# The first experts' tile table computed earlier and partly on GpSimd, its second running sum as one scan, one routing step moved by four slots and one load cut in three

## The chip, the cores and the metric

The kernel runs on one core of one Trainium2 chip. Its engines are TensorE (PE in the rows, its weight loads PEld), VectorE (DVE), ScalarE (ACT), GpSimd (POOL) and SyncE (SP, which issues most of the DMAs). The metric is the time of one execution in device microseconds, as the median of several runs: 1346.81 us for the kernel before (3 runs, 1345.29 to 1347.44).

## The reference

One decoder layer in fp32 on x of 4 x 512 x 256, with a context of 4 x 1601 x 256. Cut to what matters:

```python
x = x + self_attention(layernorm(x))            # 16 heads of 64, causal, with a relative bias
x = x + cross_attention(layernorm(x), context)  # 16 heads of 16, 1601 keys, RMS-normed q and k
# mixture of experts on h = layernorm(x), 2048 tokens
scores = softmax(h @ classifier.T)              # 40 classes: 32 experts and 8 of which each passes h on
top6 = top_k(scores + correction_bias, 6)       # six classes a token
for e in range(32):
    y[e] = (silu(h @ Wg[e].T) * (h @ Wu[e].T)) @ Wd[e].T
x = x + 2.5 * (sum over a token's experts of scores * y, and h * sum of its passing classes' scores)
```

## The kernel before

The three stages run one after the other, and each engine has its own program, written out in order; semaphores tie them. Nothing is scheduled by a planner at run time: what stands earlier on an engine is done earlier, and a wait holds all that stands behind it.

**Cross attention.** Each batch of 512 tokens takes 52 slots: 4 groups of 4 heads by 13 blocks of 128 keys. In slot s PE multiplies scores for slot s (L1226), then probabilities by values for slot s - 2 (L1241), then does one side job that a list gives the slot (PLAN, or ROUTE in the last two batches); ACT takes the exponential of the slot's scores in two pieces (L1387). At the end of a group DVE copies the sums out of PSUM (L1660), PE transposes them (L1153, side job "o"), DVE divides (L1586, L1590), and POOL adds them to x (L1063). PE's side job waits for the copy of the group before.

**Routing beside it.** While the last batch is in cross attention, the tokens of batches 0 to 2 are routed in side jobs (ROUTE): "rx" transposes the normalised tokens (L1160), "rl" multiplies them by the classifier (L1169), "rk" ranks each token within its expert (L1177, L1179). DVE normalises (L91 to L99), picks six classes (L1480 to L1507), and packs the rows with places and weights (L1513 to L1530, the function pack). POOL then sends the packed rows to HBM, sorted by expert, in 24 indirect DMAs a batch (L1033), in the order of the slots.

**The experts.** Batch 3 can be routed only when its cross attention has ended. That is the stretch on which most of the change bears: layer norm on DVE, transposes (L1964) and classifier (L1970) on PE, softmax and top six on DVE and ACT, the mask of picked classes (L2111), running counts over the four blocks of 128 tokens (L2120), two sums over the partitions on PE (L1975 for batches 0 to 2, L1976 for all), and from these the tile table. The expert stage works on 128 tiles of 128 rows; the first 40 (EARLY) hold rows of batches 0 to 2 alone, so they can start while batch 3's rows are still being sent. DVE works out for each tile its expert and its first row: tiles per expert, running sums over the 32 experts by five shifted additions (L2138), and then, one tile to a partition, the entry of the table (L2143 to L2166). PE spreads it (L1984), and DVE writes it as integers, "steer" (L2169). Only then does SP load rows (L1886 reads the table, L1887 loads). DVE packs batch 3's rows after that (L2176 to L2189), and POOL sends them (L1946).

keep_busy is a number of matmuls (L1957) whose result nobody reads. SP loads the last expert weights when x is complete (L1856, L1873). In the tile loop PE turns a tile (L1995), multiplies (L2007, L2016), with copies and silu on ACT (L2054, L2061, L2076), products on DVE (L2209, L2216), and an indirect DMA of the result by POOL (L1938). Six row tiles may be under way (X_RING). At tile 40 SP waits until batch 3's rows are sent and loads the tokens of batches 0 to 2 (acc, L1881), which are needed only at the end, when the six parts of each token are summed.

## Time and profile before

| | |
|---|---|
| median of 3 runs | 1346.81 us |
| the profiled execution | 1349.23 us |
| its span, first to last instruction | 1347.5 us |
| mean granted clock of TensorE in it | 0.972 of full speed |
| self attention, then cross attention, until | 1061.8 us |
| routing of batch 3, until the table is there | 1086.4 us |
| tile loop, until | about 1300 us |
| sums and output, until | 1347.5 us |
| busy share of PE, DVE, ACT, POOL | 91%, 53%, 64%, 52% |

The limits of the stages were read from the timeline. The clock columns are the share of full speed that was granted to TensorE: 1.00 is 2.4 GHz and 0.50 is 1.2 GHz. A row of a timeline gives start, duration, engine, line and operation, and in brackets how long the engine had been idle and for whom it waited. The whole profile's busy shares say little here: the routing of batch 3 is a chain of short instructions on one engine after the other, in which no engine but PE, with its keep_busy, looks busy.

### The profile page before, as it was taken

To read this page: it belongs to the slowest core of one execution; us is meant where nothing else is said; L and a number is where in the kernel's file an instruction comes from. 1 tells how busy PE (TensorE), PEld (TensorE's weight loads), DVE (VectorE), ACT (ScalarE), POOL (GpSimd) and SP (SyncE) were. 2 spreads that over 40 slices of the span, in tenths; PEclk is the share of its full clock that TensorE was granted. 3 is DMA by queue.
4 is the path that set the end of the run, shared out by engine and by line. 5 is a ranking of instruction groups with operands and counts; after the bars stand their busy time and mean duration, and the time that the engine had idled before them with its cause. 6 is when DMAs were issued, how large, how long until landed. Compare 5 with 4: busy or idle time off the path is not lost.

```text
span 1347.5 us, 27953 instructions
## 1 busy us (share of the span) xinstructions
PE 1232.5 (91%) x8788; PEld 761.1 (56%) x8788; DVE 716.3 (53%) x2370; ACT 865.8 (64%) x1691; POOL 695.8 (52%) x775
## 2 busy tenths in 40 slices
PE   5999999999999885899999999999989899899955
PEld 4666776776676474433333333333322589799954
DVE  6666466557555557563136313632553366566647
ACT  4666456546645425668977897789989447577730
POOL 1776557557656602355217611762377447766640
PEclk9999999999999897999999999999999889899988
DMA  7976466556535621100011001010283646665649
GB/s 238 351 253 223 166 231 229 204 175 232 184 140 193 201 63 34 33 23 12 18 40 35 9 17 40 11 35 1 94 294 123 245 141 201 223 185 177 179 152 385
DMA packets 146277, 195.08 MB, mean 145 GB/s; under 512 B 12592, under 2 KB 133056, under 8 KB 145488
## 3 DMA queue, kind: packets, MB, share of 16 engines
q1 hardware_dynamic: 135376, 162.97, 36.5%
q0 software_dynamic: 10752, 30.26, 6.3%
q8 instruction: 77, 1.26, 0.4%
q14 instruction: 72, 0.59, 0.2%
HBM read 71.01 MB, written 122.18 MB: 143 GB/s over the span
## 4 chain that ended last, share of the span: by engine, by line
PE 55%; ACT 16%; issue 12%; DVE 8%; DMA 3%; POOL 3%; ACTq 2%; SPq 0%; POOLq 0%; DVEq 0%
PE sa_pf L347 11%; ACT xa_probs L1387 8%; PE xa_banks L1226 7%; PE xa_banks L1241 6%; PE sa_po L422 5%; PE sa_ps L396 5%; PE xa_banks L1109 5%; PE sa_ptr L407 5%; PE sa_pf L380 4%; ACT mo_xs_t L2054 3%; DMA mo_w_all<-parts 2%; ACTq L2058 2%; PE mo_banks L2007 2%; ACT mo_silu L2076 1%; PE mo_banks L1957 1%
## 5 line engine op out<-in xcount | busy, mean ns | idle before, releaser
L1387 ACT ACTIVATE xa_probs<-xa_banks 128x1024 f32<-128x1024 f32 (+1 forms) x416 | 401.9, 1045 | 85.8 <-PE xa_banks L1226 84.9
L334 POOL TENSOR_SCALAR sa_probs<-sa_probs,sa_recip 128x128 f32<-128x128 f32 (+3 forms) x256 | 274.8, 1087 | 176.4 <-DVE sa_recip L585 176.2
L465 ACT ACTIVATE sa_probs<-sa_probs,sa_neg_max 128x128 f32<-128x128 f32 (+3 forms) x256 | 141.9, 555 | 148.0 <-DVE sa_neg_max L522 148.0
L1241 PE MATMUL xa_banks<-xa_probs,xa_v_one 128*17 128x512 f32 (+1 forms) x1664 | 219.6, 600 | 6.8 <-ACT xa_q_aug L1333 4.5
L1226 PE MATMUL xa_banks<-xa_q_aug,xa_k_aug 32*128 32x512 f32 (+1 forms) x1664 | 153.8, 443 | 13.6 <-issue 3.7
L1938 POOL DMA_INDIRECT parts<-mo_y,mo_dest x128 | 122.9, 960 | 61.8 <-issue 33.1
L2007 PE MATMUL mo_banks<-mo_xs_t,mo_gu 128*128 128x128 f32 x1024 | 138.5, 279 | 0.0
L522 DVE CUSTOM_DVE_ANT_0 sa_probs<-sa_ps,sa_toeplitz 128x128 f32<-128x128 f32 (+3 forms) x256 | 115.5, 488 | 38.7 <-PE sa_ps L396 35.9
L2007 PEld LDWEIGHTS mo_banks<-mo_xs_t,mo_gu 128*128 128x128 f32 x1024 | 128.0, 196 | 0.1
L2061 ACT ACTIVATE mo_gu<-mo_w_all 128x512 f32 x128 | 80.7, 630 | 67.6 <-issue 53.4
L1226 PEld LDWEIGHTS xa_banks<-xa_q_aug,xa_k_aug 32*128 32x128 f32 (+1 forms) x1664 | 62.0, 180 | 107.3 <-ACT xa_probs L1387 74.6
L582 DVE COPY sa_pt<-sa_ptr 128x128 f32<-128x128 f32 (+3 forms) x128 | 62.8, 490 | 103.8 <-PE sa_ptr L407 103.7
L407 PE MATMUL sa_ptr<-sa_ident,sa_probs 128*128 128x128 f32 x640 | 94.8, 276 | 6.7 <-ACT sa_pt L488 3.5
L407 PEld LDWEIGHTS sa_ptr<-sa_ident,sa_probs 128*128 128x128 f32 x640 | 75.7, 141 | 30.1 <-issue 11.5
L1033 POOL DMA_INDIRECT rows<-xa_k_area,xa_place_i x72 | 70.9, 985 | 38.4 <-issue 20.7
L969 POOL TENSOR_TENSOR xa_k_area<-xa_k_area 128x256 f32<-128x256 f32 (+1 forms) x39 | 23.9, 612 | 123.3 <-DVE xa_k_area L1558 115.8
L422 PE MATMUL sa_po<-sa_pt,sa_v 128*64 128x256 f32 (+3 forms) x512 | 85.2, 455 | 1.0 <-issue 1.0
L2016 PE MATMUL mo_banks<-mo_w_all,mo_hidden_t 128*128 x256 | 76.9, 383 | 0.4 <-DVE mo_y L2216 0.4
L1241 PEld LDWEIGHTS xa_banks<-xa_probs,xa_v_one 128*17 128x17 f32 (+1 forms) x1664 | 28.0, 95 | 85.3 <-issue 53.5
L1558 DVE TENSOR_TENSOR xa_k_area<-xa_banks,xa_bkv 128x256 f32<-128x256 f32 (+1 forms) x52 | 21.9, 424 | 101.0 <-PE xa_banks L1109 100.7
L488 ACT ACTIVATE sa_pt<-sa_ptr 128x128 f32<-128x128 f32 (+3 forms) x128 | 54.9, 429 | 32.1 <-PE sa_ptr L407 30.4
L2209 DVE TENSOR_TENSOR mo_hidden_t<-mo_banks,mo_silu 128x128 f32<-128x128 f32 x128 | 37.3, 291 | 71.5 <-ACT mo_silu L2076 66.7
(309 smaller groups left out, 2310.9 us busy)
## 6 DMA issues: line engine op xcount, KB each, us to landing
rows<-sa_blank SPq DMA_DIRECT2D x128, 548.0 KB, 3.5
mo_xs<-rows SPq DMA_DIRECT2D x128, 137.0 KB
parts<-sa_blank SPq DMA_DIRECT2D x96, 128.0 KB, 3.6
mo_w_all<-parts SPq DMA_DIRECT2D x16, 768.0 KB, 14.5
xa_raw<-in_ctx_t SPq DMA_DIRECT2D x24, 256.0 KB, 2.8
mo_w_all<-in_gate_up_p SPq DMA_DIRECT2D x2, 2816.0 KB, 17.2
sa_toeplitz<-extended_bias SPq DMA_DIRECT2D x8, 512.0 KB, 7.4
mo_w_all<-in_down_p SPq DMA_DIRECT2D x2, 2048.0 KB, 15.5
```

Of the source, the lines that this page charges most:

```text
L334: pool.tensor_scalar(probs[:, t % SLOTS, 0:w], probs[:, t % SLOTS, 0:w], recip[:, col:col + 1], None, ALU.mult).then_inc(probs_ready, 1)
L347: last = pe.matmul(out, u, v, start=(n == 0), stop=(n == 3 * chunks - 1))
L407: last = pe.transpose(ptr[t % 2][:, k * P:(k + 1) * P], probs[:, t % SLOTS, k * P:(k + 1) * P], ident[:])
L422: last = pe.matmul(po[a * DH:(a + 1) * DH, k * P:T], v_sb[:, k, h * DH:(h + 1) * DH], pt[:, pt_at(h, k, k):pt_at(h, k, TT)], start=(k == 0 ...
L465: act.activation(probs[:, t % SLOTS, 0:w], probs[:, t % SLOTS, 0:w], ACT.Exp, bias=neg_max[:, i:i + 1], scale=-1.0, accum_out=sums[:, i:i ...
L522: dve.tensor_tensor_reduce(out=probs[:, t % SLOTS, 0:w], in0=ps[t % SCORES][:, 0:w], in1=toeplitz[:, h, w - 1::-1], scale=-1.0 / DH, scala ...
L1226: last = pe.matmul(banks[0:m, 2 * ((n + i // 2) % 3) + i % 2, :], keys, q[rows, :], start=(k == 0), stop=(k == len(parts) - 1))
L1241: last = pe.matmul(banks[32 * i:32 * i + XD + 1, 6 + group % 2, :], v_one[b % 2][0:m, c, 4 * g + i, :], probs[0:m, (2 * j + i // 2) % RING ...
L1387: act.activation(probs[0:m, n % RING, :, :], banks[0:m, 2 * (n % 3):2 * (n % 3) + 2, :], ACT.Exp).then_inc(probs_ready, 1)
L1938: pool.indirect_dma_start(out=parts, out_offset=bass.IndirectOffsetOnAxis(ap=dest[:, t:t + 1], axis=0), in_=y[t % Y_RING][:], in_offset=No ...
L2007: last = pe.matmul(banks[:, 2 + t % 2, half * P:(half + 1) * P], gu[t % W_RING][:, at:at + INTER], xs_t[t % T_RING][:, c, :], start=(c == ...
L2061: act.activation(gu[t % W_RING][:], w_all[:, bass.ds(e * (KD * 2 * INTER), KD * 2 * INTER)], ACT.Copy).then_inc(gu_ready, 1)
```

## The change

- The side job "rk" of batch 1 moves from slot 15 to slot 19 of the last batch.
- The very last addition of the cross attention to x moves from POOL to DVE.
- PE transposes batch 3's raw tokens as soon as x is complete, and no longer the normalised ones. The mean is taken out afterwards, as mean times the column sum of the classifier (class_mean), and the factor rstd is applied after the largest logit is subtracted. The normalised rows are made by normalise(t), in four pieces put at other places.
- Everything in the tile table that depends on batches 0 to 2 alone moves from DVE to a new function on POOL, early_tiles, of 24 chained steps, whose input is summed by PE and copied by ACT beforehand.
- The total counts are summed by PE from the mask and the earlier counts in five accumulating matmuls, so that they don't wait for the running counts. The running sum of all tiles is one tensor_tensor_scan. What is left on DVE of the tile table is a short chain that joins both halves.
- The steering table is released before row_no is made. ACT runs one silu on a single column beforehand.
- acc is loaded in three parts, at tiles 56, 72 and 88, in place of one at tile 40.
- The numbers of keep_busy matmuls change: 24, 20, 26 and 12 before; 3, 2, 20, 8 and 16 now.

Cut to its core:

```diff
-             (B - 1, 10): ("rl", 1, 0), (B - 1, 15): ("rk", 1, 0), (B - 1, 22): ("rx", 2, 0),
+             (B - 1, 10): ("rl", 1, 0), (B - 1, 19): ("rk", 1, 0), (B - 1, 22): ("rx", 2, 0),
...
+                        if g == QUADS * B - 1:
+                            continue
...
+                    if group == QUADS * B - 1:
+                        wait_out(dve, f)
+                        cols = x_sb[:, :, (QUADS - 1) * 4 * XD:]
+                        dve.tensor_tensor(cols, cols, o_norm[:].rearrange("p t j d -> p t (j d)"), ALU.add
+                                          ).then_inc(x2_part, 1)
...
+    TOKENS_AT = {56: 0, 72: 1, 88: 2}
...
                 if t == EARLY:
                     sp.wait_ge(sent[1], 16 * TT * TOP_K)
-                    sp.dma_start(acc[:], x2.rearrange("b (t p) d -> p (b t) d", p=P)[:, 0:TT * LAST, :]
+                if t in TOKENS_AT:
+                    b = TOKENS_AT[t]
+                    sp.dma_start(acc[:, TT * b:TT * (b + 1), :], x2[b].rearrange("(t p) d -> p t d", p=P)
                                  ).then_inc(acc_in, 16)
...
+        def early_tiles(pool):
+            chain = Chain(pool, early_ready)
+            late = is_late[:].to_broadcast([P, E_ROUTED])
+            pool.memset(choice[:, :, E_ALL:], HUGE)
+            for i in range(3):
+                pool.memset(early_n[i][:, 0:ZEROS], 0.0)
+                last = pool.memset(all_n[i][:, 0:ZEROS], 0.0)
+            chain.then_wait(last)
+            pool.tensor_copy(counted[:, 0, :], picked[:].bitcast(F32))
+            chain.then_wait(pool.tensor_copy(meta[:, :, 2, :], spare_no[:]))
+            filled_n = early_n[2][:, ZEROS:]
+            pool.wait_ge(early_out, 1)
+            chain.then_wait(pool.tensor_scalar(counts[:], counts[:], 0.5 - 0.5 * P, TO_TILES, ALU.add, ALU.add))
+            chain.then_wait(pool.tensor_scalar(filled_n, counts[:], TO_TILES, 1.0 / P, ALU.subtract, ALU.mult))
+            held = early_n[2]
+            for i in range(5):
+                at = ZEROS - 2 ** i
+                chain.then_wait(pool.tensor_tensor(early_n[i % 2][:, ZEROS:], held[:, ZEROS:],
+                                                   held[:, at:at + E_ROUTED], ALU.add))
+                held = early_n[i % 2]
+            filled = held[:, ZEROS:]
+            chain.then_wait(pool.tensor_scalar(taken[:], filled, float(EARLY), None, ALU.min))
...
+            chain.then_wait(pool.tensor_scalar(early_steps[:], swap[:], float(P), float(REGION), ALU.mult, ALU.add))
...
+            return chain.n
...
         def run_gpsimd(pool):
+            kept.through(pool)
+            kept.stored(pool)
+            assert early_tiles(pool) == EARLY_STEPS
             pool.wait_ge(row_ready, 1)
...
             pe.wait_ge(const_ready, 2)
-            keep_busy(24)
-            pe.wait_ge(xn_ready, 1)
+            kept.sent_ready(pe)
+            pe.matmul(banks[:, 2, 0:E_ROUTED], ones_r[:], picked[:, 0:E_ROUTED], start=True, stop=True
+                      ).then_inc(early_psum, 1)
+            pe.wait_ge(kept.router_in, 32)
+            for c in range(KD):
+                last = pe.matmul(banks[:, 5, 0:E_ALL], ones[:], kept.cls[:, c, :], start=(c == 0), stop=(c == KD - 1))
+            last.then_inc(early_psum, 1)
+            keep_busy(3)
+            kept.through(pe)
...
+            act.wait_ge(const_ready, 2)
+            act.activation(silu[0][:, 0:1], ident[:, 0:1], ACT.Silu)
...
+            for t in range(TT):
+                last = dve.bn_stats(stats[:, t, :], own_x[:, t, :])
+            chain.then_wait(last)
+            for t in range(TT):
+                last = dve.bn_aggr(mean_var[:, t, :], stats[:, t, :])
+            chain.then_wait(last)
+            dve.wait_ge(early_psum, 2)
+            dve.tensor_tensor(class_mean[:], banks[:, 5, 0:E_ALL].unsqueeze(1).to_broadcast([P, TT, E_ALL]),
+                              mean_var[:, :, 0:1].to_broadcast([P, TT, E_ALL]), ALU.mult)
+            chain.then_wait(dve.tensor_scalar(var[:], mean_var[:, 0:TT, 1], LN_EPS, None, ALU.add))
+            rsqrt(dve, chain, rstd[:], var[:], tmp[:])
+
             dve.wait_ge(lg_psum, 1)
             logits = banks[:, 4, 0:TT * E_ALL].rearrange("p (t e) -> p t e", e=E_ALL)
-            chain.then_wait(dve.tensor_reduce(tmp[:], logits, AX.X, ALU.max))
-            dve.tensor_tensor(scores[:], logits, tmp[:].unsqueeze(2).to_broadcast([P, TT, E_ALL]), ALU.subtract
+            chain.then_wait(dve.tensor_tensor(scores[:], logits, class_mean[:], ALU.subtract))
+            chain.then_wait(dve.tensor_reduce(row_max[:], scores[:], AX.X, ALU.max))
+            chain.then_wait(dve.tensor_tensor(scores[:], scores[:], row_max[:].unsqueeze(2)
+                                              .to_broadcast([P, TT, E_ALL]), ALU.subtract))
+            dve.tensor_tensor(scores[:], scores[:], rstd[:].unsqueeze(2).to_broadcast([P, TT, E_ALL]), ALU.mult
                               ).then_inc(shifted, 1)
+            normalise(0)
...
+            dve.wait_ge(early_ready, 2)
...
+            dve.tensor_tensor(mask[:], left[:, :, 0:E_ALL], choice[:, :, 0:E_ALL], ALU.not_equal
+                              ).then_inc(mask_ready, 1)
+            dve.wait_ge(mask_ready, 1)
+            for t in range(TT - 1):
                 last = dve.tensor_tensor(counted[:, t + 1, :], counted[:, t, :].bitcast(F32),
                                          mask[:, t, :].bitcast(F32), ALU.add)
-                if t == TT - 1:
-                    last.then_inc(mask_ready, 1)
-                else:
+                if t < TT - 2:
                     chain.then_wait(last)
+            last.then_inc(counted_ready, 1)
+
+            n_tiles = all_n[2][:, ZEROS:]
+            dve.wait_ge(count_psum, 1)
+            chain.then_wait(dve.tensor_scalar(ends[:], banks[:, 7, 0:E_ROUTED], 0.5 * P - 0.5, TO_TILES,
+                                              ALU.add, ALU.add))
+            chain.then_wait(dve.tensor_scalar(n_tiles, ends[:], TO_TILES, 1.0 / P, ALU.subtract, ALU.mult))
+            all_tiles = all_n[0][:, ZEROS:]
+            chain.then_wait(dve.tensor_tensor_scan(all_tiles, ones[:, 0:E_ROUTED], n_tiles, 0.0, ALU.mult, ALU.add))
+            dve.wait_ge(early_ready, EARLY_STEPS)
+            dve.scalar_tensor_tensor(out=steps[:], in0=n_tiles, scalar=late_rows[:], in1=early_steps[:],
+                                     op0=ALU.mult, op1=ALU.add)
+            chain.then_wait(dve.scalar_tensor_tensor(out=ends[:], in0=all_tiles, scalar=is_late[:],
+                                                     in1=early_ends[:], op0=ALU.mult, op1=ALU.add))
+            chain.then_wait(dve.tensor_scalar(below[:, 1, :], ends[:], tile_no[:], None, ALU.is_le))
+            chain.then_wait(dve.tensor_tensor(below[:, 0, :], below[:, 1, :], steps[:], ALU.mult))
+            chain.then_wait(dve.tensor_reduce(found[:], below[:], AX.X, ALU.add))
+            chain.then_wait(dve.tensor_tensor(found[:], found[:], first_row[:], ALU.add))
+            chain.then_wait(dve.tensor_tensor(at_e[:], found[:], caps[:], ALU.min))
+            dve.tensor_tensor(diag[:], ident[:].unsqueeze(1).to_broadcast([P, 2, P]),
+                              at_e[:].unsqueeze(2).to_broadcast([P, 2, P]), ALU.mult).then_inc(diag_ready, 1)
+            normalise(1)
             dve.scalar_tensor_tensor(out=weights[:], in0=mask[:].bitcast(F32), scalar=ROUTE_SCALE, in1=scores[:],
                                      op0=ALU.mult, op1=ALU.mult)
...
             dve.wait_ge(diag_psum, 1)
-            dve.tensor_copy(steer[:], banks[0:1, 5, 0:2 * N_TILES])
-            dve.tensor_scalar(row_no[:], banks[:, 5, 0:N_TILES], tile_no[:], None, ALU.add
-                              ).then_inc(steer_ready, 1)
-            dve.wait_ge(steer_ready, 1)
+            dve.tensor_copy(steer[:], banks[0:1, 5, 0:2 * N_TILES]).then_inc(steer_ready, 1)
+            chain.then_wait(dve.tensor_scalar(row_no[:], banks[:, 5, 0:N_TILES], tile_no[:], None, ALU.add))
+            normalise(2)
+            normalise(3)
```

On DVE, around slots 14 to 19 of the last batch, before (xa_o is the copy of the group's sums, xa_k_area and xa_q_lo here hold the packed rows and scratch of pack, xa_xn the raw tokens of batch 2):

```order
L1660 COPY xa_o<-xa_banks 128x512 [waits xa_pv_done]
L1513 TENSOR_TENSOR xa_raw<-xa_banks,xa_k_area 128x160 [waits xa_prep_psum]
...
L1530 TENSOR_REDUCE xa_k_area<-xa_q_lo 128x4x6
L1586 RECIPROCAL xa_rec<-xa_banks 128x16 [waits xa_prep_psum]
L1590 TENSOR_TENSOR xa_o_norm<-xa_banks,xa_rec 128x256 [waits xa_x2_part,xa_dve_chain]
L91 BN_STATS xa_stats<-xa_xn 128x6 [waits xa_xr_in2]
...
L99 TENSOR_SCALAR xa_k_area<-xa_xn,xa_mean_var,xa_rstd 128x256 x3
L1541 COPY xa_xt<-xa_banks 128x512 [waits xa_prep_psum] x2
```

and in the change (lines of the changed file):

```order
L1667 COPY xa_o<-xa_banks 128x512 [waits xa_pv_done]
L1588 RECIPROCAL xa_rec<-xa_banks 128x16 [waits xa_prep_psum]
L1592 TENSOR_TENSOR xa_o_norm<-xa_banks,xa_rec 128x256 [waits xa_x2_part,xa_dve_chain]
L91 BN_STATS xa_stats<-xa_xn 128x6 [waits xa_xr_in2]
...
L99 TENSOR_SCALAR xa_k_area<-xa_xn,xa_mean_var,xa_rstd 128x256 x3
L1515 TENSOR_TENSOR xa_raw<-xa_banks,xa_k_area 128x160 [waits xa_prep_psum]
...
L1532 TENSOR_REDUCE xa_k_area<-xa_q_lo 128x4x6
L1543 COPY xa_xt<-xa_banks 128x512 [waits xa_prep_psum] x2
```

The packing of batch 1 now stands behind the normalising of batch 2 and directly ahead of the two copies of batch 2's transposes.

On POOL, at the end of the cross attention, before:

```order
L1033 DMA rows<-xa_k_area,xa_place_i 77953x274 x11
L1063 TENSOR_TENSOR xa_x<-xa_x,xa_o_norm 128x4x64 [waits xa_prep_out,xa_prep_out_act]
L1946 DMA rows<-mo_packed,mo_place_i 77953x274 [waits mo_row_ready]
```

and in the change:

```order
L1033 DMA rows<-xa_k_area,xa_place_i 77953x274 x11
L1964 MEMSET mo_choice 128x4x2 [waits xa_xr_out,xa_x2_part]
L1966 MEMSET mo_early_n 128x16
...
L1970 COPY mo_packed<-mo_spare_no 128x4x6
L1973 TENSOR_SCALAR mo_counts<-mo_counts 128x32 [waits mo_early_out,mo_early_ready]
L1974 TENSOR_SCALAR mo_early_n<-mo_counts 128x32 [waits mo_early_ready]
L1978 TENSOR_TENSOR mo_early_n<-mo_early_n 128x32 [waits mo_early_ready] x5
...
L1997 TENSOR_SCALAR mo_first_row<-mo_first_row 128x1 [waits mo_early_ready]
L2017 DMA rows<-mo_packed,mo_place_i 77953x274 [waits mo_row_ready,mo_early_ready]
```

Between the last row sent and the first of batch 3 there was one addition; now there are the 31 instructions of early_tiles, which cannot start before the sending is over.

On DVE, from the counts to the diagonal that PE spreads, in the change (before, 27 instructions stood here, L2130 to L2166 of the listing above):

```order
L2221 TENSOR_SCALAR mo_ends<-mo_banks 128x32 [waits mo_count_psum]
L2223 TENSOR_SCALAR mo_all_n<-mo_ends 128x32 [waits mo_dve_chain]
L2225 SCALAR_TENSOR_TENSOR mo_all_n<-mo_ones,mo_all_n 128x32 [waits mo_dve_chain]
L2227 SCALAR_TENSOR_TENSOR mo_steps<-mo_all_n,mo_late_rows,mo_early_steps 128x32 [waits mo_early_ready,mo_dve_chain]
L2229 SCALAR_TENSOR_TENSOR mo_ends<-mo_all_n,mo_is_late,mo_early_ends 128x32
L2231 TENSOR_SCALAR mo_below<-mo_ends,mo_tile_no 128x32 [waits mo_dve_chain]
L2232 TENSOR_TENSOR mo_below<-mo_below,mo_steps 128x32 [waits mo_dve_chain]
L2233 TENSOR_REDUCE mo_found<-mo_below 128x2 [waits mo_dve_chain]
L2234 TENSOR_TENSOR mo_found<-mo_found,mo_first_row 128x2 [waits mo_dve_chain]
L2235 TENSOR_TENSOR mo_at_e<-mo_found,mo_caps 128x2 [waits mo_dve_chain]
L2236 TENSOR_TENSOR mo_diag<-mo_ident,mo_at_e 128x256 [waits mo_dve_chain]
```

L2225 is the scan; L2227 is where DVE waits for the last of POOL's 24 steps.

## Rows read from the trace of the kernel before

**Rows 1.** Timeline of ACT, last batch; start us, us, instruction [idle before <-releaser]

```profile
986.00 1.94 ACT L1387 ACTIVATE xa_probs<-xa_banks 128x1024 f32<-128x1024 f32 x2 [3.01 <-PE xa_banks L1226]
988.71 1.94 ACT L1387 ACTIVATE xa_probs<-xa_banks 128x1024 f32<-128x1024 f32 x2 [0.76 <-PE xa_banks L1226]
990.94 9.33 ACT L1387 ACTIVATE xa_probs<-xa_banks 128x1024 f32<-128x1024 f32 x10 [0.29 <-PE xa_banks L1226]
```

**Rows 2.** Timeline of PE, last batch

```profile
984.39 0.31 PE L1177 MATMUL xa_banks<-xa_ct_hi 128*128 128x160 f32 x1 [2.38 <-DVE xa_o L1660]
...
1001.44 0.66 PE L1160 MATMUL xa_banks<-xa_ident,xa_k_area 128*128 128x128 f32 x4
...
1007.34 1.98 PE L1169 MATMUL xa_banks<-xa_k_area,xa_xt 128*128 128x40 f32 x16
```

**Rows 3.** Timeline of DVE, last batch

```profile
984.85 0.33 DVE L1513 TENSOR_TENSOR xa_raw<-xa_banks,xa_k_area 128x160 f32<-128x160 f32 x1 [0.67 <-PE xa_banks L1179]
...
990.27 0.26 DVE L1586 RECIPROCAL xa_rec<-xa_banks 128x16 f32<-128x16 f32 x1 [0.25 <-PE xa_banks L1153]
...
995.93 1.55 DVE L99 TENSOR_SCALAR xa_k_area<-xa_xn,xa_mean_var,xa_rstd 128x256 f32<-128x256 f32 x4
```

**Rows 4.** Timeline of POOL, last batch and after

```profile
997.98 0.96 POOL L1033 DMA_INDIRECT rows<-xa_k_area,xa_place_i  x1 [0.30 <-issue]
...
1059.92 0.96 POOL L1033 DMA_INDIRECT rows<-xa_k_area,xa_place_i  x1 [0.30 <-issue]
1061.10 0.72 POOL L1063 TENSOR_TENSOR xa_x<-xa_x,xa_o_norm 128x256 f32<-128x256 f32 x1 [0.22 <-DVE xa_o_norm L1590]
```

**Rows 5.** Timeline of DVE, routing of batch 3

```profile
1061.85 1.40 DVE L91 BATCH_NORM_STATS2 mo_stats<-xa_x 128x6 f32<-128x256 f32 x4 [0.91 <-POOL xa_x L1063]
...
1072.12 0.33 DVE L2094 TENSOR_REDUCE mo_tmp<-mo_banks 128x4 f32<-128x160 f32 x1 [4.56 <-PE mo_banks L1970]
...
1075.92 0.32 DVE L2111 TENSOR_TENSOR mo_mask<-mo_left,mo_choice 128x160 fp32r<-128x160 f32 x1
...
1079.16 0.19 DVE L2130 TENSOR_SCALAR mo_counts<-mo_banks 128x32 f32<-128x32 f32 x1 [1.29 <-PE mo_banks L1976]
...
1084.50 0.42 DVE L2166 TENSOR_TENSOR mo_diag<-mo_ident,mo_at_e 128x256 f32<-128x256 f32 x1
...
1086.06 0.33 DVE L2170 TENSOR_SCALAR mo_row_no<-mo_banks,mo_tile_no 128x128 f32<-128x128 f32 x1
```

**Rows 6.** Timeline of PE, routing of batch 3 and first tile

```profile
1069.25 2.83 PE L1970 MATMUL mo_banks<-xa_k_area,mo_xt 128*128 128x40 f32 x16 [0.83 <-ACT mo_xt L2046]
1071.88 7.11 PE L1957 MATMUL mo_banks<-mo_ident 128*128 128x128 f32 x40
1078.75 0.26 PE L1975 MATMUL mo_banks<-mo_counted,mo_ones_r 128*128 128x32 f32 x1
...
1092.63 1.92 PE L2007 MATMUL mo_banks<-mo_xs_t,mo_gu 128*128 128x128 f32 x8
```

**Rows 7.** Groups by line and form: busy us, mean ns | idle before

```profile
L1914 POOL CAST mo_region_at<-mo_numbers 128x32 f32<-128x32 int32 x1 | 0.2, 209 | 0.1
L2248 DVE TENSOR_TENSOR mo_acc<-mo_acc,mo_w_all 128x256 f32<-128x256 f32 x8 | 3.4, 425 | 0.3
```

**Rows 8.** Stretches: length, busy (x) of PE, PEld, DVE, ACT, POOL; clock, DMA, GB/s

```profile
1070.00:1072.00 2.00, 2.00 (x12) 2.00 (x11) 0.00 (x0) 0.00 (x0) 0.00 (x0) 0.53 0.97 418
...
1078.00:1080.00 2.00, 2.00 (x20) 2.00 (x20) 0.73 (x5) 0.00 (x0) 0.00 (x0) 1.00 0.65 270
```

**Rows 9.** Timeline of SP, row loads before tile 40

```profile
1130.87 17.23 SPq L1887 DMA_DIRECT2D mo_xs<-rows  x12
```

**Rows 10.** Chain of waits: start us, us, what

```profile
1149.42 8.49 DMA mo_xs<-rows
```

**Rows 11.** Timeline of PE, tiles 40 and 42

```profile
1157.95 0.69 PE L1995 MATMUL mo_banks<-mo_ident,mo_xs 128*128 128x128 f32 x2 [4.58 <-DMA mo_xs<-rows]
...
1163.15 0.38 PE L1995 MATMUL mo_banks<-mo_ident,mo_xs 128*128 128x128 f32 x2
```

157 lines of the change are left out of this document (71 added, 86 removed).

## The prediction

> **What bounds the kernel now.** I read the chain of waits first, then the timelines of the engines in the three stretches that the change touches. There are three holes.
>
> In the last batch of cross attention ACT sets the pace: ten exponentials take 9.33 us, so a slot of two takes 1.87 us [rows 1]. PE keeps just ahead of it. At slot 15 PE's side job "rk" needs the copy xa_o, which on DVE stands behind the choice of classes for batch 1; PE stands idle for 2.38 us [rows 2], and ACT starves for 3.01 us and then, while PE catches up, for 0.76 us [rows 1].
>
> The routing of batch 3 is a pure chain, from the complete x at 1061.85 to the released table at 1086.39 (the end of row_no) [rows 5], and the first tile's product starts at 1092.63 [rows 6]. Nothing else can be done meanwhile, so what leaves this chain leaves the time.
>
> In the tile loop twelve row loads are issued in 17.23 us, (17.23 - 0.35) / 11 = 1.535 us a tile, with PE full [rows 9]. At tile 40 the acc load of 1.5 MB is ahead of the rows in SP's queue: these rows take 8.49 us to land [rows 10], and PE idles 4.58 us; then two tiles take 1163.15 - 1157.95 = 5.20 us where 3.07 are normal, 2.1 us more [rows 11].
>
> **Slot 15.** Without "rk" there, PE needs xa_o only at slot 17, for "o". The idle times 3.01 + 0.76 fall to about nothing, the 0.29 of slot 17 stays: -3.75 us. The step is now at slot 19, and its packing on DVE stands behind the normalising of batch 2. From the start of the pack at 984.85 to the end of the normalising at 995.93 + 1.55 = 997.48 is 12.63 us, 0.25 of them idle [rows 3]. Now PE's heads are there 3.75 us earlier, at 990.27 - 3.75 = 986.5, and DVE does division, normalising and pack in 12.4 us, until 998.9. The copy of batch 2's first transposes stands behind that and takes 0.7 us. PE's second transposes (slot 23) would start at 1001.44 - 3.75 = 997.7 [rows 2] and need the bank that this copy empties: at 999.6. PE stands for 1.9 us, at a place where ACT has no more slack than its 0.3 us a side job. Some of the normalising rows are stretched, so the cost lies between 0 and 1.9; I take 1.9. Cross attention then ends 1.85 us earlier.
>
> POOL is not paced by slots: it sends row after row without a gap, 0.96 + 0.30 = 1.26 us each. The first row of batch 1 goes at 997.98 and must now wait for that pack, about 1.2 us, which is not made up. Its last send ends at 1059.92 + 0.96 + 1.2 = 1062.1 [rows 4]. SP needs the rows only with the table, 10 us later: hidden.
>
> **x complete.** The last addition took POOL from 1061.10 to 1061.82 behind a division that ended at 1060.94 [rows 4]. DVE does it right behind the division in 0.425 us [rows 7], by 1061.43: -0.4. So x is complete at T0 = 1061.43 - 1.85 = 1059.6.
>
> **Layer norm, transposes, classifier.** Before, they follow one another: 1072.12 - 1061.85 = 10.27 us [rows 5]. Now PE goes T0 + 0.05, transposes and ACT copies 1.92, classifier 1.98 at full clock (as in the last batch, rows 2) or 2.83 as here [rows 6]: T0 + 3.95 to 4.8. DVE beside it goes through the statistics (1.40 us, rows 5), the aggregates and the root (13 instructions of a few columns at 0.1 to 0.2 us) in 4.0 us, and class_mean adds 0.36: T0 + 4.4. The later of both, 4.5 us: -5.8. Behind it come two more DVE instructions of 0.36 us: +0.7. normalise(0) lies under the exponential on ACT.
>
> The clock was granted in full until 1070, then at 0.53 [rows 8], after PE had been idle for 0.83 us ahead of the classifier [rows 6] and longer ahead of the transposes; it is at its lower level, 1.2 GHz, for most of the next 6 us. Now both gaps shrink to 0.5 us or less, so I take the full clock.
>
> **Mask to counts.** From the end of the mask, 1076.24, to the first count on DVE at 1079.16 are 2.9 us [rows 5]. It was bounded by PE: its 40 instructions of keep_busy at the lower clock took 7.11 us and ended when L1975 could start [rows 6]. At full clock, 20 in 2 us [rows 8], they take 4 to 4.6 us and end before the mask. Then five matmuls, 0.41 + 3 x 0.11, and the wake-up: 0.8 us. -2.1.
>
> **The table.** 1084.92 - 1079.16 = 5.76 us before [rows 5]. What is left on DVE, by the same kinds of instruction there (0.21 to 0.28 us from start to start): two on the counts 0.44, the scan 0.27, seven from the join to at_e 1.6, diag 0.42: 2.73 us, -3.0. The scan is in no row; it lies between 0.2 us (a 32-column instruction) and the 1.26 us of the five additions that it replaces; it is near the first. The Trainium skill (DVE: opcode table, instruction layouts, handler registers and perf-mode slots, section Datapath and trigger behaviour) says that the scan runs at half throughput; by this 32 columns would gain an estimated 0.03 us, and nothing else would change. The table is released by the copy to steer and no longer by row_no: -0.3.
>
> Sum of the chain: -0.4 - 5.8 + 0.7 - 2.1 - 3.0 - 0.3 = -10.9.
>
> **POOL's half.** It must be there when DVE has scanned, at T0 + 4.5 + 1.9 + 3.0 + 0.8 + 0.7 = T0 + 10.8 = 1070.4. POOL starts at 1062.1. Seven memsets and two copies, none over 0.21 us [rows 7] and partly overlapping, take about 1.5 us. Of the 22 chained steps, ten have one input or one column, 0.21 us [rows 7] plus 0.07 to the next; twelve have two inputs of 32 columns, which no row shows: not under 0.21 and not over the 0.72 of 256 columns [rows 4]. I take 0.26: 10 x 0.28 + 12 x 0.33 = 6.8. Ready at 1070.4, a tie: +0.3 for the spread. By the upper bound it would be +5.
>
> The Trainium skill (GPSIMD Engine Reference, section Engine selection) speaks against such a move: elementwise work with two inputs is to go to VectorE, GpSimd being about twice as slow. The trace has 0.72 against 0.425 us at 256 columns [rows 4, 7]. By that rule a step would be an estimated 0.4 us, and DVE would wait about 1.5 us more; the sum would be 1.5 us worse.
>
> **Weights.** They are requested when x is complete. The traffic ended near 1079.3 [rows 8], 17.5 us later, and was hidden behind a table at 1086.4. Now x comes 2.3 us earlier and the table at 1086.4 - 10.9 - 1.85 + 0.3 = 1073.9; weights land near 1077.3, while the first rows, queued behind them, land near 1077.5. The first tile needed 6.2 us from the table [rows 5, 6], so 1080.1. Nearly hidden: +0.5.
>
> The packing of batch 3's rows follows the table and gets 0.7 us longer by normalise(2) and (3): about 1079.8, before the first gate at 1081.5. Hidden.
>
> **Tile 40.** 4.58 + 2.1 = 6.7 us go. Each of the three new loads is a third of the bytes; 8.49 us were some 6.4 more than a usual landing, so a third costs 2.1 us of lateness against a lead of about 3.8 us less a landing of 2.1: 0.3 to 0.4 each. +0.9. Net -5.8.
>
> **Sum.** -1.85 - 10.9 + 0.3 + 0.5 - 5.8 = -17.75 us, against the profiled execution's 1349.23: 1331.5. That execution was 2.4 us above the median of 1346.81, so 1329.1 for the median. I predict 1329.
>
> **Rivals.**
>
> (a) The handed-over steps come late. For: two-input steps are priced by no row. Against: the one-input ones. With the twelve at 0.6 to 0.7 us, near the upper bound, DVE waits 4 us: 1333. Chance 0.13.
>
> (b) PE's clock falls to 1.2 GHz in this stretch all the same. For: it did before. Then the classifier takes 0.4 us more and keep_busy(20) lasts until T0 + 11.9 where the mask is there at T0 + 9.4: 1332. Chance 0.12.
>
> (c) Weights are late. Their traffic now competes with 2 us of POOL's sends and the first rows; 3 us later than I place them would show as 2 to 3: 1331.5. Chance 0.1.
>
> (d) The pack at slot 19 doesn't hold PE, and the three small loads fit into the ring: 1.9 + 0.9 less, 1326. Chance 0.12.
>
> (e) Slower than before: POOL takes, for each of the 22 steps, what its instructions in rows 4 take from start to start, 1.265 us. Then its half is ready at 1062.1 + 1.5 + 27.8 = 1091.4, 21 us behind DVE, which eats the whole gain of 17.75: 1350. It decides from 1.13 us a step. Against: casts of 32 columns at 0.21 [rows 7]. Chance 0.02. The move might also miss its aim in part, if DVE were held at slot 17 by something else: that is inside the range.
>
> The forecast itself, 1327 to 1331, has 0.5. 1323.5 to 1335 leaves less than 0.2 outside. A change of under 0.2%, 2.7 us, can't be told from none; faster by more 0.96, within 0.02, slower 0.02.
>
> **What would show it.** In the profile after: ACT without a gap at slot 15 and one of about 2 us near slot 23; DVE's first statistics 0.4 us behind its last division; from there to the scores 4.5 us; one wait of DVE on POOL at the join, under 1 us; the table about 12.5 us earlier than at 1086.4; the first product about as much earlier; no idle time of PE at tile 40, and small ones at 56, 72 and 88. I am wrong if PE's clock column stands at 0.5 in the routing, if POOL's steps are over 0.4 us, or if ACT's first weight copy stands behind the DMA.

## The result, and the profile after

The changed kernel takes 1334.36 us (median of 4 runs, 1333.03 to 1337.21), the kernel before 1347.12 us beside it (4 runs, 1345.29 to 1348.94): ratio 0.9908, 95% interval 0.9886 to 0.9930. That is 12.8 us faster. Forecast was 1329.0, within 1327 to 1331 with a chance of 0.5, and with a range of 1323.5 to 1335: the sign and the range hold, the narrower stretch doesn't, and the gain is 5 us smaller than the forecast one.

The profiled executions are 1349.23 (before) and 1333.03 us (after), their spans 1347.5 and 1331.1: 16.4 us less. The spans taken apart at four marks that both traces have (x complete is the start of the first statistics of batch 3, a tile's product is the start of its gate and up matmuls; the table is row_no before and steer after):

| stretch | before | after | difference | forecast |
|---|---|---|---|---|
| start of the kernel to x complete | 1061.85 | 1059.27 | -2.58 | -2.25 |
| x complete to the released table | 24.54 | 14.31 | -10.23 | -10.2 |
| table to the first tile product | 6.24 | 9.17 | +2.93 | +0.5 |
| first product to the last one | 204.79 | 197.14 | -7.65 | -5.8 |
| last product to the end | 50.08 | 51.21 | +1.13 | 0 |

**The last batch of cross attention.** The timeline of ACT (start us, duration us, instruction, in brackets idle before it):

```profile
977.38 9.34 ACT L1389 ACTIVATE xa_probs<-xa_banks 128x1024 f32<-128x1024 f32 x10
987.02 9.52 ACT L1389 ACTIVATE xa_probs<-xa_banks 128x1024 f32<-128x1024 f32 x10 [0.30 <-PE xa_banks L1228]
996.84 1.94 ACT L1389 ACTIVATE xa_probs<-xa_banks 128x1024 f32<-128x1024 f32 x2 [0.30 <-PE xa_banks L1228]
1000.51 5.61 ACT L1389 ACTIVATE xa_probs<-xa_banks 128x1024 f32<-128x1024 f32 x6 [1.73 <-PE xa_banks L1228]
```

Ten exponentials run through slot 15, where there were 3.01 and 0.76 us of idle time [rows 1]; a new wait of 1.73 us has come at slot 23. PE stands there for it:

```profile
999.18 0.63 PE L1162 MATMUL xa_banks<-xa_ident,xa_k_area 128*128 128x128 f32 x4 [1.39 <-issue]
```

The same on DVE, the end of the packing of batch 1 and the copy that frees the bank, is the hold that the prediction placed here:

```profile
997.33 1.14 DVE L1532 TENSOR_REDUCE xa_k_area<-xa_q_lo 128x24 f32<-128x960 f32 x1
998.40 0.68 DVE L1543 COPY xa_xt<-xa_banks 128x512 f32<-128x512 f32 x1
```

**The routing.** DVE from x complete to the table (answers to [rows 5]):

```profile
1058.81 0.42 DVE L1598 TENSOR_TENSOR xa_x<-xa_x,xa_o_norm 128x256 f32<-128x256 f32 x1
1059.27 1.41 DVE L2174 BATCH_NORM_STATS2 mo_stats<-xa_x 128x6 f32<-128x256 f32 x4
...
1063.76 0.32 DVE L2187 TENSOR_TENSOR mo_scores<-mo_banks,mo_class_mean 128x160 f32<-128x160 f32 x1
...
1068.30 0.33 DVE L2209 TENSOR_TENSOR mo_mask<-mo_left,mo_choice 128x160 fp32r<-128x160 f32 x1
...
1069.51 0.19 DVE L2221 TENSOR_SCALAR mo_ends<-mo_banks 128x32 f32<-128x32 f32 x1 [0.18 <-PE mo_banks L2056]
...
1069.95 0.22 DVE L2225 TENSOR_TENSOR_SCAN mo_all_n<-mo_ones,mo_all_n 128x32 f32<-128x32 f32 x1
1070.36 0.25 DVE L2227 SCALAR_TENSOR_TENSOR mo_steps<-mo_all_n,mo_late_rows,mo_early_steps 128x32 f32<-128x32 f32 x1 [0.18 <-POOL mo_first_row L1997]
...
1073.17 0.41 DVE L2242 CAST mo_steer<-mo_banks 1x256 int32<-1x256 f32 x1 [0.23 <-PE mo_banks L2066]
```

From the first statistics to the scores are 4.49 us (forecast 4.5), from the end of the mask to the first count 0.88 (0.8), from there to the end of diag (1071.96 + 0.42) 2.87 (2.73). The wait at the join with POOL's half is there and is 0.18 us. PE ran this whole stretch at the full clock (granted 1.00 in every 2 us from 1060 to 1080):

```profile
1061.12 1.98 PE L2048 MATMUL mo_banks<-xa_k_area,mo_xt 128*128 128x40 f32 x16 [0.29 <-ACT mo_xt L2130]
1062.93 4.71 PE L2028 MATMUL mo_banks<-mo_ident 128*128 128x128 f32 x40
1068.77 0.25 PE L2054 MATMUL mo_banks<-mo_counted,mo_ones_r 128*128 128x32 f32 x1 [1.14 <-POOL mo_swap L1992]
```

Before, the classifier took 2.83 us and the forty instructions 7.11 [rows 6].

**The first tile.** The weights in the chain of waits (start us, us, what), then ACT, then PE:

```profile
1060.26 20.06 DMA mo_w_all<-in_down_p
```

```profile
1081.25 0.63 ACT L2147 ACTIVATE mo_gu<-mo_w_all 128x512 f32 x1 [14.21 <-DMA mo_w_all<-in_down_p]
```

```profile
1080.79 1.01 PE L2077 MATMUL mo_banks<-mo_ident,mo_xs 128*128 128x128 f32 x4 [4.09 <-DMA mo_xs<-rows]
...
1082.75 1.48 PE L2089 MATMUL mo_banks<-mo_xs_t,mo_gu 128*128 128x128 f32 x6
```

The weights landed at 1080.3. In the chain of waits of before this load doesn't occur; here it is the step of 20.06 us that replaces the routing. Two stretches, with the columns of [rows 8]:

```profile
1062.00:1064.00 2.00, 2.00 (x19) 2.00 (x19) 1.69 (x10) 0.00 (x0) 1.66 (x12) 1.00 0.89 299
1078.00:1080.00 2.00, 0.00 (x0) 0.00 (x0) 1.55 (x4) 0.00 (x0) 0.00 (x0) 1.00 0.86 285
```

In the first one, beside POOL's steps, the DMA engines are 89% busy and move only 299 GB/s, where from 1068 to 1078 they move 405 to 442; in the second one PE and ACT have no instruction at all and wait for transfers, while POOL waits for DVE's packing of batch 3.

**The loop.** SP's queue around the first of the three smaller loads: the whole load is gone from tile 40, and PE has no idle time there. Behind the first part (1161.00) no tile is longer by more than 0.04 us; behind the second (1186.23) one tile is longer by 0.27, behind the third (1210.79) two by 0.25 and 0.33 us.

```profile
1074.63 86.33 SPq L1910 DMA_DIRECT2D mo_xs<-rows  x56
1161.00 0.44 SPq L1904 DMA_DIRECT2D mo_acc<-x  x1
1162.89 23.30 SPq L1910 DMA_DIRECT2D mo_xs<-rows  x16
```

**The end.** The last stretch is 1.1 us longer, and all of it is one wait of DVE, for one of the last loads of the tokens' parts: the instruction ahead of it stands at the same place in both stretches, to within 0.05 us. Before, then after:

```profile
1339.20 0.96 DVE L2245 TENSOR_TENSOR mo_w_all<-mo_w_all 128x768 f32<-128x768 f32 x1 [0.73 <-DMA mo_w_all<-parts]
```

```profile
1322.83 0.96 DVE L2317 TENSOR_TENSOR mo_w_all<-mo_w_all 128x768 f32<-128x768 f32 x1 [1.93 <-DMA mo_w_all<-parts]
```

The experiments below ran on other chips, where every kernel took about 9% longer, the kernel before too (1470 to 1478 us). So their times stand only beside each other and as ratios to before, each pinned to about 0.2 to 0.3% (3 to 4 us); below that I read the stretch from x complete to the first product in each trace. One condition is different there. In the traces of the first chip POOL's row sends ran until 1.0 us ahead of x complete (before) and 2.67 us behind it (after, 1061.94 against 1059.27). In all twelve traces of the other chips they had ended 11.7 to 15.1 us ahead of it, as here, where x was complete at 1115.95 (changed kernel, second trace):

```profile
1103.29 0.96 POOL L1033 DMA_INDIRECT rows<-xa_k_area,xa_place_i  x1 [0.30 <-issue]
```

So the experiments don't contain the part of the weights' lateness that comes from the sends.

### The profile page after: what moved, and what is told of

The parts are those of the page before. It is cut to its first block, busy times and chain, and to the rows that moved or that the text cites. A ratio compares the mean times of both kernels' runs of the same rounds, so it can differ in the third digit from the quotient of the medians.

```text
span 1331.1 us, 27858 instructions
## 1 busy us (share of the span) xinstructions
PE 1220.5 (92%) x8730; PEld 748.9 (56%) x8730; DVE 714.2 (54%) x2347; ACT 867.6 (65%) x1693; POOL 704.9 (53%) x810
## 3 DMA queue, kind: packets, MB, share of 16 engines
q8 instruction: 77, 1.26, 0.4%
## 4 chain that ended last, share of the span: by engine, by line
PE 62%; ACT 13%; issue 9%; DVE 7%; DMA 4%; POOL 3%; ACTq 1%; SPq 0%; POOLq 0%; DVEq 0%
PE sa_pf L347 11%; ACT xa_probs L1389 8%; PE xa_banks L1228 7%; PE xa_banks L1243 6%; PE mo_banks L2089 6%; PE sa_po L422 5%; PE sa_ps L396 5%; PE xa_banks L1111 5%; PE sa_ptr L407 5%; PE sa_pf L380 4%; PE mo_banks L2098 3%; DMA mo_w_all<-parts 2%; DMA mo_w_all<-in_down_p 2%; PE mo_banks L2077 1%; ACT mo_xs_t L2140 1%
```

## Experiments

| run | ratio to before (95%) | us from x complete to: table | first product |
|---|---|---|---|
| the changed kernel again | 0.9905 (0.9884 to 0.9926) | 14.12 | 21.92 |
| weights early, three runs | 0.9859, 0.9876, 0.9875 | 14.11, 14.11, 14.11 | 20.22, 20.25, 20.15 |
| five additions | 0.9895 (0.9874 to 0.9916) | 15.00 | 21.44 |
| five additions, weights early | 0.9891 (0.9870 to 0.9911) | 14.99 | 21.09 |
| routing alone | 0.9938 (0.9913 to 0.9962) | 14.12 | 22.03 |
| slot 19 alone | 0.9979 (0.9961 to 0.9997) | 22.82 | 29.29 |
| before, weights early | 1.0014 (0.9989 to 1.0039) | 24.28 | 30.82 |
| acc whole | 0.9917 (0.9888 to 0.9946) | 14.11 | 22.13 |
| rx at 24 and 25, weights early, two runs | 0.9893, 0.9865 | 14.13, 14.55 | 20.28, 20.66 |

(Table here is the end of the copy to steer, in every kernel; in the first two traces it is 24.28 and 14.31, and the first product 30.78 and 23.48.)

**The changed kernel again.**

> The changed kernel once more, nothing edited, for a tighter interval. If the two traces tell the truth about the change, it is 16.4 us faster than before (ratio 0.9878). If part of those 16.4 us is run-to-run spread, it is the 12.8 us of the first medians (0.9905). The stretch from the last product to the end, 51.2 us after against 50.1 before, differs between runs if it is spread, and stays at 51.2 if the change causes it.

0.9905 is the first ratio again (0.9908), and 0.9878 lies just outside its interval. In microseconds, of 1469.87, it is 14.0 us less (10.9 to 17.1), and which scale holds on a chip that is 9% slower is not known; so it leans to 12.8 and doesn't exclude 16.4. The last stretch is 51.8 us here. It was 51.2 to 53.6 in the eleven traces with the new routing, and 50.1, 51.1 and 50.7 in the three with the old one. The one wait of DVE shown above is clearer: 1.81 to 2.18 us in all eleven, 0.72 to 0.74 in all three. So some 1.1 us of it belongs to the change, and to its routing, since it is there with slot 15 and the whole acc load put back (routing alone). Why that load lands later stays open.

**Weights early.** The second part of the weights is requested when the last product with V is done:

```diff
-            kept.through(sp)
+            kept.multiplied(sp)
             load_weights(sp, FIRST_WEIGHTS, E_ROUTED)
+        def multiplied(eng):
+            eng.wait_ge(pv_done, B * SLOTS)
```

> The changed kernel, with the last gate/up weights and the down weights requested after the last product with V (about 1056.4 us in its trace) and not after x is complete (1059.2). Theory W (the landing of the weights at 1080.3 sets the first tile): they land 2 to 2.8 us earlier, the first tile product moves from 1082.75 to between 1080.0 and 1080.7, and the time falls by 2.0 to 2.7 us against the changed kernel. Rival R (the first tile is set by the table at 1073.6 plus the time its own rows take): no change, within 0.5 us. Rival C (the weights then compete with the row sends of POOL and with the last chain): the sends' landings get longer, and less than 1 us is gained.

> The changed kernel with the weights requested after the last product with V, run again. In the first run the weights landed 17.6 us after x was complete (20.5 in the changed kernel beside it), the first product came 1.7 us earlier from there, and the medians differed by 5.3 us with 3 us of uncertainty. Theory W2: the weights gave 1.7 us and the third row load, behind which PE's first product stands, is the next bound: 1.7 to 2.0 us less than the changed kernel (1332.5 where that has 1334.4). Theory W (all of the lateness comes back): 2.6 us less. Rival: more than 3 us, so that something beyond the first tile gets shorter too.

> Early weights a third time, for the size of the gain and a trace. Against before, the changed kernel's ratio is 0.9905 and 0.9908 and that of early weights 0.9859 and 0.9876. Theory W2 (the third row load is the next bound) gives 1.7 us less than the changed kernel, a ratio of 0.9892; that more than the first tile gets shorter would show as 0.987 or less again. In the trace the first product comes 20.2 us after x is complete, the table 14.1.

From the trace of the second run, PE and ACT at the first tile:

```profile
1138.63 0.41 PE L2080 MATMUL mo_banks<-mo_ident,mo_xs 128*128 128x128 f32 x2 [0.60 <-DMA mo_xs<-rows]
1139.61 0.44 PE L2080 MATMUL mo_banks<-mo_ident,mo_xs 128*128 128x128 f32 x2 [0.56 <-DMA mo_xs<-rows]
1140.78 0.44 PE L2080 MATMUL mo_banks<-mo_ident,mo_xs 128*128 128x128 f32 x2 [0.74 <-DMA mo_xs<-rows]
1141.05 1.06 PE L2092 MATMUL mo_banks<-mo_xs_t,mo_gu 128*128 128x128 f32 x8
```

```profile
1138.65 0.63 ACT L2150 ACTIVATE mo_gu<-mo_w_all 128x512 f32 x1 [10.14 <-DMA mo_w_all<-in_down_p]
```

Requested 2.8 us earlier, the weights landed 2.7 to 3.0 us earlier (ACT's first copy 17.59, 17.85 and 17.81 us after x complete, 20.55 in the changed kernel's second trace), and the first product came 1.7 us earlier, 6.1 us behind the table (6.5 in before with early weights). What bounds it now is visible: three row loads, one behind the other, the third ahead of the first product in PE's order. Theory W2 holds up to the first product; rivals R and C fall.

In the time the three runs average 0.9870 against 0.9905 and 0.9908, some 5 us with about 3 of uncertainty: an improvement on both kernels, and somewhat more than 1.7. The traces show where more comes from, as the rival of the second run has it. The two tiles behind the first product took 2.22, 2.27 and 2.28 us with early weights, and 3.78 in the changed kernel's second trace, so that 1.5 us more are gained there, 3.2 in all. The granted clock differs, first that kernel, then early weights (columns of [rows 8]):

```profile
1138.00:1140.00 2.00, 2.00 (x11) 2.00 (x10) 0.00 (x0) 1.16 (x4) 1.39 (x3) 0.50 0.76 198
```

```profile
1141.00:1143.00 2.00, 2.00 (x20) 1.99 (x19) 0.84 (x5) 1.12 (x4) 1.11 (x1) 1.00 0.48 126
```

PE had been idle for 2.83 us ahead of its first tile in the one, for 0.60, 0.56 and 0.74 us in the other. That early weights keep the clock is not shown by this: with five additions it is the other way round (1.00 with late weights, 0.50 with early ones).

**Before, with its weights early.** The same edit in the kernel before.

> The kernel before, with its weights requested after the last product with V, 2.8 us earlier. Theory W (the landing only counts where it is later than the table): the table of before comes 24.3 us after x is complete and the weights 17.5, so nothing follows: equal within 0.2% (1 to 2 us of the noise of these runs). Rival C (the weights' traffic in itself slows the last batch or the routing, so that its place matters): a difference of 2 us or more, of either sign.

1.0014: no difference, to within 0.25% (3.7 us). In the trace, which is finer, the first product comes 30.82 us after x complete, 30.78 in before. The request moved by 3.1 us here, since x is completed by POOL. The same transfer, moved by about as much, is worth nothing under a table at 24.3 us and 1.7 us under one at 14.1. That is the step of the prediction that mattered.

**Five additions in place of the scan**, without and with early weights:

```diff
-            chain.then_wait(dve.tensor_tensor_scan(all_tiles, ones[:, 0:E_ROUTED], n_tiles, 0.0, ALU.mult, ALU.add))
+            held = all_n[2]
+            for i in range(5):
+                at = ZEROS - 2 ** i
+                chain.then_wait(dve.tensor_tensor(all_n[i % 2][:, ZEROS:], held[:, ZEROS:],
+                                                  held[:, at:at + E_ROUTED], ALU.add))
+                held = all_n[i % 2]
```

> The changed kernel with the five shifted additions of 32 columns in place of the scan. Theory W: the table comes 1.0 us later (five steps of 0.25 us for 0.27, less 0.18 of waiting for POOL that goes), and nothing follows, since the weights land 6.7 us behind the table: time equal within 0.4 us. Rival R: the first tile is 1.0 us later, and so is the end.

> The early weights with the five shifted additions in place of the scan. The weights no longer cover the table, so if the table sets the first row loads, the 0.8 us by which five additions made the table later now shows in the first product and in the time: 0.8 us slower than early weights with the scan. If the weights still set the first product, both are equal.

DVE in the run with early weights; the scan in the other kernel with early weights:

```profile
1129.73 1.10 DVE L2231 TENSOR_TENSOR mo_all_n<-mo_all_n 128x32 f32<-128x32 f32 x5
1130.86 0.25 DVE L2235 SCALAR_TENSOR_TENSOR mo_steps<-mo_all_n,mo_late_rows,mo_early_steps 128x32 f32<-128x32 f32 x1
```

```profile
1131.42 0.23 DVE L2228 TENSOR_TENSOR_SCAN mo_all_n<-mo_ones,mo_all_n 128x32 f32<-128x32 f32 x1
1131.68 0.25 DVE L2230 SCALAR_TENSOR_TENSOR mo_steps<-mo_all_n,mo_late_rows,mo_early_steps 128x32 f32<-128x32 f32 x1
```

From start to start five additions are 1.13 us, the scan 0.26: 0.87 us. The table came 0.88 us later in both. Under late weights the first product did not follow, 21.44 against 21.92: the row loads were asked for 0.88 us later, and the weights landed 1.0 us earlier (ACT's first copy at 19.51 and 20.55). With early weights it did follow, 21.09 against 20.25. So the scan, by itself, was worth nothing measurable in the changed kernel as it stands, and 0.8 us once the weights are out of the way. The medians (0.9895 and 0.9905; 0.9891 and 0.9876) agree but can't show it alone; the second pair holds 1.6 us of clock as well (the two tiles behind the first product 3.83 us against 2.27).

**Routing alone**: rk back at slot 15, acc whole at tile 40.

```diff
-             (B - 1, 10): ("rl", 1, 0), (B - 1, 19): ("rk", 1, 0), (B - 1, 22): ("rx", 2, 0),
+             (B - 1, 10): ("rl", 1, 0), (B - 1, 15): ("rk", 1, 0), (B - 1, 22): ("rx", 2, 0),
-    TOKENS_AT = {56: 0, 72: 1, 88: 2}
+    TOKENS_AT = {40: 0}
```

> The changed kernel with two parts undone: the step rk of batch 1 back at slot 15 and the acc load whole at tile 40. What is left is the work on the routing of batch 3. My sum on record gives 10.1 us faster than before for it. By the trace of the changed kernel it is 7.7 us up to the first product and 1.1 in the first tiles: 8.8 us faster than before, and 8.2 us slower than the changed kernel (2.2 for slot 15, 6.0 for tile 40).

0.9938 is 9.1 us on these chips; it fits 8.8, and doesn't exclude the 10.1 on record. In the stretch the table is as early as with the whole change (14.12) and the first product 8.8 us earlier than in before (30.8 to 22.0). For this stretch the sum has 9.7; its other 0.4 lies ahead of x complete.

**Slot 19 alone**, in the kernel before.

> The kernel before, with nothing changed but the step rk of batch 1 moved from slot 15 to slot 19. On record: ACT's idle 3.75 us of slot 15 goes, slot 23 holds PE for 1.9 us, net 1.85 us faster. By the trace of the changed kernel the hold is 1.4 us and the net 2.24 us. x complete moves from 1061.85 to 1059.6, the first tile product from 1092.63 to about 1090.4 (there the table sets it), and the time falls by 1.9 to 2.3 us. Rival: the hold at slot 23 eats all of it, 0.

0.9979 (-3.1 us; -0.4 to -5.7) excludes the rival, narrowly, and not more. The trace brought something that I had not asked: the table came 22.82 us after x complete, where it was 24.28 in before and in before with early weights. PE in the two, first this kernel, then that one:

```profile
1130.12 5.92 PE L1957 MATMUL mo_banks<-mo_ident 128*128 128x128 f32 x40
1135.93 0.28 PE L1975 MATMUL mo_banks<-mo_counted,mo_ones_r 128*128 128x32 f32 x1
```

```profile
1135.17 7.25 PE L1960 MATMUL mo_banks<-mo_ident 128*128 128x128 f32 x40
1142.17 0.26 PE L1978 MATMUL mo_banks<-mo_counted,mo_ones_r 128*128 128x32 f32 x1
```

The same forty instructions that hold the counts took 1.33 us less because the clock was back earlier (the granted clock is 0.96 from 1132.5 to 1134.5 here, 0.50 from 1137.3 to 1139.3 there, the same place in the chain), and the table came 1.46 us earlier. It is the "mask to counts" term in an unplanned trial: in before, that part of the chain was PE at its lower level. Whether the move of the step or the chance of one execution brought the clock back is not shown by one trace each; so the 3.1 us are no clean measure of slot 19.

**acc whole**, nothing else undone:

> The changed kernel with the acc load whole again at tile 40. On record the whole load costs 6.7 us and the three parts 0.9, net 5.8 us. By the two traces 6.9 and 0.85, net 6.0. So 5.8 to 6.0 us slower than the changed kernel (1340.3 where that has 1334.4), with PE idle for 4.5 us at tile 40 and two slower tiles behind. Rival: the parts cost as much as the whole where rows land late anyway, less than 2 us.

```profile
1247.97 0.69 PE L2076 MATMUL mo_banks<-mo_ident,mo_xs 128*128 128x128 f32 x2 [5.17 <-DMA mo_xs<-rows]
1248.45 1.91 PE L2088 MATMUL mo_banks<-mo_xs_t,mo_gu 128*128 128x128 f32 x8
1251.43 1.42 PE L2088 MATMUL mo_banks<-mo_xs_t,mo_gu 128*128 128x128 f32 x8
1253.34 1.06 PE L2088 MATMUL mo_banks<-mo_xs_t,mo_gu 128*128 128x128 f32 x8
```

The hole is back, with its slow tiles: from product to product 7.15, 2.98 and 1.91 us, 7.4 more than three tiles of 1.545 (6.9 in the first chip's trace of before). The kernel's ratio, 0.9917, is 0.0012 above the changed one's with 0.0036 of uncertainty: the time by itself doesn't settle 5.8 against under 2, the trace does at its place.

**Transposes of batch 2 at 24 and 25**, with early weights:

```diff
-             (B - 1, 10): ("rl", 1, 0), (B - 1, 19): ("rk", 1, 0), (B - 1, 22): ("rx", 2, 0),
-             (B - 1, 23): ("rx", 2, 1), (B - 1, 26): ("rl", 2, 0), (B - 1, 32): ("rk", 2, 0)}
+             (B - 1, 10): ("rl", 1, 0), (B - 1, 19): ("rk", 1, 0), (B - 1, 24): ("rx", 2, 0),
+             (B - 1, 25): ("rx", 2, 1), (B - 1, 26): ("rl", 2, 0), (B - 1, 32): ("rk", 2, 0)}
```

> Early weights, and the transposes of batch 2 moved from slots 22 and 23 to 24 and 25, behind DVE's packing of batch 1. If the packing holds PE at slot 23 in the changed kernel, ACT's wait of 1.73 us there goes back to 0.3, x is complete 1.4 us earlier and the time is 1.4 us below early weights alone. Rival: the copies and the packing of batch 2 then come too late for its choice of classes at slot 28, and the hold only moves: 0.

> Early weights with the transposes of batch 2 at slots 24 and 25, again, beside early weights alone on the same chip. If the packing's hold at slot 23 sets the end of the last batch, 1.4 us less than early weights alone and no wait of ACT above 0.4 us between the slots 17 and 26. If other waits take its place (the first run showed no hold there, and no gain in the time: 0.9893 against 0.9876), equal within 1 us.

ACT over the slots 21 to 26, in the third run of early weights and in the second of this kernel:

```profile
1008.68 5.64 ACT L1389 ACTIVATE xa_probs<-xa_banks 128x1024 f32<-128x1024 f32 x6 [0.31 <-PE xa_banks L1228]
1014.62 1.94 ACT L1389 ACTIVATE xa_probs<-xa_banks 128x1024 f32<-128x1024 f32 x2 [0.30 <-PE xa_banks L1228]
1017.17 1.94 ACT L1389 ACTIVATE xa_probs<-xa_banks 128x1024 f32<-128x1024 f32 x2 [0.61 <-PE xa_banks L1228]
1019.67 1.93 ACT L1389 ACTIVATE xa_probs<-xa_banks 65x1024 f32<-65x1024 f32 x2 [0.57 <-PE xa_banks L1228]
```

```profile
1009.46 9.34 ACT L1389 ACTIVATE xa_probs<-xa_banks 128x1024 f32<-128x1024 f32 x10 [0.32 <-PE xa_banks L1228]
1019.06 1.02 ACT L1389 ACTIVATE xa_probs<-xa_banks 65x1024 f32<-65x1024 f32 x1 [0.25 <-PE xa_banks L1228]
```

Ten exponentials take 9.60 us to the next start where they took 10.99: the hold is gone there, 1.39 us. In the time it can't be seen (0.9893 and 0.9865 beside 0.9876 and 0.9875 on the same chips). On these chips ACT stands for far longer elsewhere in the same batch, as the last section shows, so whether the 1.4 us reach the end stays open.

## Why the prediction was right and where it was not

- **Slot 15.** Right. 3.75 us of idle time went, the hold at slot 23 came, 1.4 us at PE and 1.73 at ACT where I had taken 1.9; the end of the batch moved by 2.24 us (o_norm 1060.52 to 1058.28), forecast 1.85. POOL's last send ended at 1061.94, forecast 1062.1. That holds for the first chip alone, as the sends of the others had ended long before.
- **x complete to the table.** Right, and by its own parts: 10.23 us measured, 10.2 in the sum (-10.9, with x complete's 0.4 taken out and POOL's 0.3 put in). Layer norm 4.49, mask to counts 0.88, the half of POOL ready at 1070.24 where 1070.4 was forecast.
- **The scan.** 0.26 us from start to start, forecast 0.27; the five additions 1.13, not 1.26. The rule of half throughput in the Trainium skill (DVE: opcode table, instruction layouts, handler registers and perf-mode slots, section Datapath and trigger behaviour) leaves no mark at this width: the scan of 32 columns takes 0.22 us, an addition of 32 columns 1.10 / 5 = 0.22.
- **POOL's steps.** The upper bound (5 us) and rival (a) are off. Steps with two inputs took 0.24 to 0.40 us, the five additions 1.54 / 5 = 0.31, against 0.22 on DVE. The estimate that went by the Trainium skill (GPSIMD Engine Reference, section Engine selection), 0.4 a step and 1.5 us of wait, was too dark at 32 columns: the wait was 0.18. It was the tie that was forecast, with the sends ending behind x complete; on the other chips, where POOL starts at x complete, its half was ready 2.7 us ahead of DVE (1128.97 against 1131.65, second run of early weights).
- **Weights.** The step that failed is "weights land near 1077.3 ... Nearly hidden: +0.5". They landed at 1080.3, and table to first product took 2.93 us more instead of 0.5. The prediction's own sign of being wrong, ACT's first weight copy behind the DMA, came true (14.21 us of wait). Two errors are in it. The 17.5 us were the end of the traffic, read from stretches of 2 us, and not the landing: the last load of before was asked for at 1062.7 and landed 17.7 us later, 18.5 us after x was complete. And I carried the duration of before over as if it were the queue's own: after, it landed 21.05 us after x was complete, 2.5 us later than before. In that time the DMA engines moved 7.81 MB, before 6.84, of which the weights are 6.82; the rest is 0.43 MB of sends and 0.53 MB of rows. At the 405 to 442 GB/s of 1068 to 1078 these 0.96 MB are an estimated 2.2 to 2.4 us, which leaves little for another cause. Rival (c) named the cause and its size (2 to 3), and had a chance of 0.1. With early weights the excess is gone in the traces of the other chips, where without the sends it was 1.3 us and not 2.7 (first product behind steer: 7.80 against 6.54 there, 9.17 against 6.50 on the first chip); on the first chip early weights were not run.
- **Tile 40.** Right: 6.9 us gone, 0.85 put back, net 6.0 (forecast 5.8); the small costs lie behind the second and third part alone, and not behind each of the three. The loop gained 1.55 us more in its first tiles, which had no term: the three tiles behind the first product took 6.06 us before and 4.51 after. The granted clock was at 0.50 from 1092 to 1096 before, and after from 1082 to 1084, with 0.92 in the next 2 us. (The 1.1 us in the expectation of routing alone is an earlier and lower reading of the same tiles.)
- **The last stretch**, +1.1 us, had no term either. It is one load that DVE waits 1.93 us for instead of 0.73, in every trace with the new routing; why it lands later was not tried.
- **The sum.** It came within 1.5 us of the profiled execution partly by luck: 2.4 us of waiting for weights and 1.1 us of the last stretch are missing from it, and so are 1.85 us that the loop gained beyond it and 0.3 us ahead of x complete.
- **From the trace to the median.** Against the profiled execution the sum said 1331.5, and 1333.03 was measured: 1.5 us off. The other 3.7 us of the miss are in the conversion: I took off 2.4 us because the profiled execution of before was above its median, and the one of after lies 1.3 us below its own. One execution stands about 2 us off its median, either way; a forecast made against one carries that.

The likeliest reason for a smaller median gain than the span's 16.4 is that spread; the second measurement, 14.0 us on a slower chip, lies between 12.8 and 16.4.

## What to carry to other kernels

When a chain is shortened, put beside its new end every transfer that it used to cover, with the traffic that is new in that window and not only the old duration, and take its landing rather than the end of its traffic: here 2.9 us of the 12.8 us that the table came earlier went into waiting for one load, and 1.7 of them could be had back on chips without the sends. A request can often go to the last reader of the bytes it overwrites rather than to the end of the stage. Once a stretch is bound by a transfer, faster instructions in it, the scan among them, show nothing until the transfer is moved.
